# Earlier pieces of a chip kernel's start: one array tile for the first convolution kernels, a shorter VectorE chain, a later x load, and the first Toeplitz rows in two pieces

## What is computed

```python
dt = exp(log_dt); A = -exp(log_A_real) + 1j * A_imag
dtA = A * dt[:, None]
P = dtA[:, :, None] * arange(1024)
Cs = Cc * (exp(dtA) - 1.0) / A
K = 2.0 * einsum('hn,hnl->hl', Cs, exp(P)).real     # filter of 1024 taps for each of 64 channels, 64 modes
y = irfft(rfft(u * mask, 2048) * rfft(K, 2048))[..., :1024] + u * mask * D[:, None]
y = y * mask
x = x + attention(y)
x = x + ffn(x @ W[condition])
```

## Time and profile before

| what | us |
|---|---|
| median of 3 runs | 920.03 |
| lowest and highest | 919.63, 921.61 |
| the profiled execution, its own time | 920.28 |
| its span (first to last instruction) | 918.5 |
| busy in the span: PE | 879.2 (96%) |
| busy in the span: DVE, POOL, ACT | 444.7, 395.0, 202.1 |
| PE at work on the convolution from | 27.3 |
| PE at work on the projections from | 179.2 |

### The profile page before, as it was taken

How to read it: one execution, slowest core, us unless ns; L and a number is a source line. 1 busy time by engine, 2 the same in 40 slices (tenths; PEclk the granted TensorE clock), 3 DMA queues, 4 the chain that set the end, 5 groups by cost and what they waited for, 6 DMA issues and landing times.

```text
span 918.5 us, 24871 instructions
## 1 busy us (share of the span) xinstructions
PE 879.2 (96%) x11040; PEld 765.9 (83%) x11040; DVE 444.7 (48%) x935; ACT 202.1 (22%) x363; POOL 395.0 (43%) x294
## 2 busy tenths in 40 slices
PE   0899999999999999999999999999999999999998
PEld 0789899988888888888777777777789999999997
DVE  7555663111222222248887766788533344333444
ACT  4334552200000000023133222333231111011110
POOL 1244555401565556759978877877521000000000
PEclk9999999999999999999999999999999999999999
DMA  2678877412213322155546463634252221212201
GB/s 65 153 189 205 202 178 185 128 46 69 69 70 92 89 72 69 47 183 155 158 117 178 115 182 115 198 113 139 97 185 95 70 93 47 93 70 70 92 26 69
DMA packets 81930, 105.35 MB, mean 115 GB/s; under 512 B 41504, under 2 KB 54432, under 8 KB 81824
## 3 DMA queue, kind: packets, MB, share of 16 engines
q1 hardware_dynamic: 81312, 103.24, 39.1%
q0 software_dynamic: 512, 0.53, 0.2%
HBM read 74.08 MB, written 29.65 MB: 113 GB/s over the span
## 4 chain that ended last, share of the span: by engine, by line
PE 92%; DMA 2%; DVE 2%; issue 1%; SPq 1%; POOL 1%; ACT 0%; DVEq 0%; POOLq 0%
PE ps L810 24%; PE ps L1262 21%; PE ps L1076 19%; PE ps L529 9%; PE ps L774 5%; PE ps L540 4%; PE ps L1032 3%; PE ps L1012 3%; PE ps L1235 2%; PE ps L1282 1%; DMA kpad<-ksb 1%; PE ps L1283 1%; DMA xc<-in_dram 1%; DMA toep<-kpad 1%; PE ps L460 0%
## 5 line engine op out<-in xcount | busy, mean ns | idle before, releaser
L1262 PE MATMUL ps<-wb,xf 128*128 128x420 f32 (+1 forms) x1152 | 195.2, 329 | 0.0
L1262 PEld LDWEIGHTS ps<-wb,xf 128*128 128x128 f32 x1152 | 189.6, 188 | 2.8 <-issue 0.2
L810 PE MATMUL ps<-y_hi,w_hi 128*128 128x512 f32 x320 | 125.2, 391 | 0.0
L810 PE MATMUL ps<-y_lo,w_hi 128*128 128x512 f32 x320 | 124.6, 390 | 0.0
L810 PE MATMUL ps<-y_hi,w_lo 128*128 128x512 f32 x320 | 124.6, 389 | 0.0
L529 PE MATMUL ps<-xc,toep 64*128 64x192 f32 (+4 forms) x1088 | 100.9, 338 | 12.8 <-DMA toep<-kpad 8.4
L529 PEld LDWEIGHTS ps<-xc,toep 64*128 64x128 f32 x1088 | 92.9, 192 | 17.0 <-issue 12.5
L1076 PE MATMUL ps<-y_hi 128*128 128x512 f32 x256 | 103.9, 406 | 0.2 <-POOL y_lo L945 0.2
L1076 PE MATMUL ps<-y_lo,y_hi 128*128 128x512 f32 x256 | 100.7, 393 | 0.0
L1076 PE MATMUL ps<-y_hi,y_lo 128*128 128x512 f32 x256 | 100.6, 393 | 0.0
L917 POOL TENSOR_TENSOR rot<-rot,cst 128x512 f32<-128x512 f32 x40 | 52.7, 1318 | 73.0 <-DVE rot L888 73.0
(11 more groups left out here) (145 smaller groups left out, 1284.9 us busy)
## 6 DMA issues: line engine op xcount, KB each, us to landing
toep<-kpad SPq DMA_DIRECT2D x64, 272.0 KB, 4.6
xc<-in_dram SPq DMA_DIRECT2D x32, 256.0 KB, 5.0
q_rows<-rf SPq DMA_DIRECT2D x32, 256.0 KB, 2.6
q<-q_rows SPq DMA_DIRECT2D x16, 512.0 KB, 5.0
xr<-in_dram SPq DMA_DIRECT2D x16, 512.0 KB, 4.6
x_scratch<-xr SPq DMA_DIRECT2D x16, 512.0 KB, 3.1
x<-x_scratch SPq DMA_DIRECT2D x16, 512.0 KB, 3.7
out_dram<-x SPq DMA_DIRECT2D x15, 512.0 KB, 2.6
```

Of the source, the lines that this page charges most:

```text
L810: mm = pe.matmul(kq_bank(n), w[a][:, j, :], yt[b][:, j, g * 512:(g + 1) * 512], start=(j == 0 and a + b == 0), stop=(j == NJ - 1 and a == 1))
L1262: mm = pe.matmul(joint_bank(i, piece)[:, 0:hi - lo], xf[i % 2][:, a, t, :], wb[t][:, w4_place(t, c), lo:hi], start=(t == 0 and a + c == 0) ...
```

## The change

Five edits, all in the convolution's first steps.

- `phase_rates`: the negation of `ar` is gone; `rho` is made by one instruction from `ar` and `dt` with the factor -1. `ar` keeps its sign, and later sums and differences are turned accordingly.
- `first_tables`: the two squares of `ar` and of the imaginary part are made by ScalarE, behind `sh` and `ch`; VectorE waits for eight of ScalarE's results rather than six, and has 22 instructions rather than 24.
- group 0 only, `kernels_pe` and `kernels_out`: two matmuls over all 128 rows into bank 6 rather than four over 64 rows into two banks; the addition of bank 7 is gone. The groups from 1 on are as before.
- `load_parameters`: x for n = 0 and 1 is loaded behind the zeros, the skip weights and the lengths.
- `load_toeplitz`: for n = 0 each of the two loads is cut in two at column 576 (`NEAR`): both near pieces first, with a semaphore of their own, then both far pieces. `convolve(0)` begins on the near pieces and waits for the far ones ahead of `narrow`.

```diff
@@ load_parameters
             sp.dma_start(cst[:], consts).then_inc(ld_cst, 16)
-            load_x_conv(sp, 0)
...
             sp.dma_start(len_i[:], lens.partition_broadcast(P)).then_inc(ld_len, 16)
+            load_x_conv(sp, 0)
@@ first_magnitudes_and_sines
             act.activation(M("ch"), M("r"), ACT.Sin, scale=0.4999998, bias=C("half_pi")).then_inc(a_set, 1)
+            act.activation(M("k"), M("ar"), ACT.Square).then_inc(a_set, 1)
+            act.activation(M("t2"), AIM, ACT.Square).then_inc(a_set, 1)
             sines(act, 0)
@@ phase_rates
             v.wait_ge(a_set, 2)
-            chain(v, v.tensor_scalar(M("ar"), M("ar"), -1.0, None, ALU.mult))
-            chain(v, v.tensor_tensor(M("rho"), M("ar"), M("dt"), ALU.mult))
+            chain(v, v.scalar_tensor_tensor(M("rho"), M("ar"), -1.0, M("dt"), ALU.mult, ALU.mult))
@@ first_tables
-            v.wait_ge(a_set, 6)
+            v.wait_ge(a_set, 8)
...
-            v.tensor_tensor(M("k"), M("ar"), M("ar"), ALU.mult)
-            chain(v, v.tensor_tensor(M("t2"), AIM, AIM, ALU.mult))
+            chain(v, v.tensor_tensor(M("k"), M("k"), M("t2"), ALU.add))
             v.scalar_tensor_tensor(M("t0"), M("cm1"), 1.0, M("tanh"), ALU.add, ALU.mult)
             v.tensor_tensor(M("ni"), M("t1"), M("e1"), ALU.mult)
-            chain(v, v.tensor_tensor(M("k"), M("k"), M("t2"), ALU.add))
-            v.tensor_tensor(M("nr"), M("t0"), M("cm1"), ALU.add)
             chain(v, v.reciprocal(M("den"), M("k")))
+            chain(v, v.tensor_tensor(M("nr"), M("t0"), M("cm1"), ALU.add))
@@ kernels_pe
-                for r in range(2):
+                if g == 0:
+                    mm = pe.matmul(ps[:, 6, cols], ltab[:, cols], rtab[:, cols], start=True, stop=True)
+                for r in range(2 if g > 0 else 0):
@@ kernels_out
-            v.tensor_copy(k, low).then_inc(v_kl, 1)
-            v.wait_ge(v_kl, g + 1)
-            v.tensor_tensor(k, k, high, ALU.add).then_inc(v_ke, 1)
+            if g == 0:
+                v.tensor_copy(k, low).then_inc(v_ke, 1)
+            else:
+                v.tensor_copy(k, low).then_inc(v_kl, 1)
+                v.wait_ge(v_kl, g)
+                v.tensor_tensor(k, k, high, ALU.add).then_inc(v_ke, 1)
@@ load_toeplitz
+        NEAR = NJ // 2 * P + HALF
...
+            near = NEAR if n == 0 else 0
+            if near:
+                for r in range(2):
+                    sp.dma_start(toep[r * HALF:(r + 1) * HALF, n % TR, 0:near],
+                                 bass.AP(kpad, head(n, r) * (KROW + 1), [[1, HALF], [1, near]])).then_inc(ld_near, 16)
             for r in range(2):
-                sp.dma_start(toep[r * HALF:(r + 1) * HALF, n % TR, :],
-                             bass.AP(kpad, head(n, r) * (KROW + 1) + 0, [[1, HALF], [1, L + HALF]])).then_inc(ld_toep[n % TR], 16)
+                sp.dma_start(toep[r * HALF:(r + 1) * HALF, n % TR, near:],
+                             bass.AP(kpad, head(n, r) * (KROW + 1) + near, [[1, HALF], [1, L + HALF - near]])).then_inc(ld_toep[n % TR], 16)
@@ convolve
-            pe.wait_ge(ld_toep[n % TR], 16 * 2 * (n // TR + 1))
+            if n == 0:
+                pe.wait_ge(ld_near, 16 * 2)
+            else:
+                pe.wait_ge(ld_toep[n % TR], 16 * 2 * (n // TR + 1))
...
                         mm = wide(pe, n, c, d, start=(d + c == 0))
+                if n == 0:
+                    pe.wait_ge(ld_toep[0], 16 * 2)
```

More of the change, by code:

```diff
@@ L260, in build @@
         st_zero, st_k = signal("st_zero"), signals("st_k", 2 * GP)
+        ld_near = signal("ld_near")
         ld_toep, ld_xc = signals("ld_toep", TR), signals("ld_xc", XR)
@@ L409, in first_tables @@
             phases(v, 0)
-            v.wait_ge(a_set, 6)
+            v.wait_ge(a_set, 8)
+            v.scalar_tensor_tensor(M("cm1"), M("sh"), -2.0, M("sh"), ALU.mult, ALU.mult)
             v.scalar_tensor_tensor(M("tanh"), M("e1"), 1.0, M("tanh"), ALU.add, ALU.mult)
-            v.scalar_tensor_tensor(M("cm1"), M("sh"), -2.0, M("sh"), ALU.mult, ALU.mult)
             v.scalar_tensor_tensor(M("t1"), M("sh"), 2.0, M("ch"), ALU.mult, ALU.mult)
-            v.tensor_tensor(M("k"), M("ar"), M("ar"), ALU.mult)
-            chain(v, v.tensor_tensor(M("t2"), AIM, AIM, ALU.mult))
+            chain(v, v.tensor_tensor(M("k"), M("k"), M("t2"), ALU.add))
             v.scalar_tensor_tensor(M("t0"), M("cm1"), 1.0, M("tanh"), ALU.add, ALU.mult)
             v.tensor_tensor(M("ni"), M("t1"), M("e1"), ALU.mult)
-            chain(v, v.tensor_tensor(M("k"), M("k"), M("t2"), ALU.add))
-            v.tensor_tensor(M("nr"), M("t0"), M("cm1"), ALU.add)
             chain(v, v.reciprocal(M("den"), M("k")))
+            chain(v, v.tensor_tensor(M("nr"), M("t0"), M("cm1"), ALU.add))
+            v.tensor_tensor(M("t1"), M("ni"), AIM, ALU.mult)
             v.tensor_tensor(M("t0"), M("nr"), M("ar"), ALU.mult)
-            v.tensor_tensor(M("t1"), M("ni"), AIM, ALU.mult)
             v.tensor_tensor(M("t2"), M("ni"), M("ar"), ALU.mult)
             chain(v, v.tensor_tensor(M("k"), M("nr"), AIM, ALU.mult))
-            v.tensor_tensor(M("gr"), M("t0"), M("t1"), ALU.add)
-            chain(v, v.tensor_tensor(M("gi"), M("t2"), M("k"), ALU.subtract))
+            v.tensor_tensor(M("gr"), M("t1"), M("t0"), ALU.subtract)
+            chain(v, v.tensor_tensor(M("gi"), M("t2"), M("k"), ALU.add))
             v.tensor_tensor(M("gr"), M("gr"), M("den"), ALU.mult)
@@ L434, in first_tables @@
             chain(v, v.scalar_tensor_tensor(M("k"), M("gr"), 2.0, CIM, ALU.mult, ALU.mult))
-            v.tensor_tensor(M("cr"), M("t0"), M("t1"), ALU.subtract)
-            chain(v, v.tensor_tensor(M("ci"), M("t2"), M("k"), ALU.add))
+            v.tensor_tensor(M("cr"), M("t0"), M("t1"), ALU.add)
+            chain(v, v.tensor_tensor(M("ci"), M("k"), M("t2"), ALU.subtract))
         def tables(v, g):
```

## The result

The changed kernel's median was 915.17 us (911.26 to 920.47, 9 runs) beside 917.82 for the kernel before (916.36 to 921.61, 9 runs): ratio 0.9964 with a 95% interval of 0.9948 to 0.9979. It is faster, by 0.36%: little, but outside the interval's noise. The forecast 917.6 lay 2.4 too high. Against the 920.03 that stood in the first table the gain is 4.86, twice what I forecast.

What follows compares the result with a forecast made beforehand. TensorE, 92% of the critical chain, was taken as the bound, so only an earlier start could help: 0.23 + 0.27 + 0.45 + 1.45 = 2.40 off the 920.03 median gives 917.6 us, range 914.9 to 920.6.

Steps and rivals of the forecast that it cites:

- Part 1: VectorE's rates: folding the negation into rho saves one waited instruction, a gain of 0.23 us.
- Part 2: Group 0's tables: moving two squares from VectorE to ScalarE saves two issue slots, 0.27 us (bounds 0.13 and 0.52).
- Part 3: Group 0's first filters: one bank without the addition gains 0.45 us; the whole-array matmuls themselves count 0.
- Part 4: Loading x behind the small loads at the start: no gain, 0 us.
- Part 5: First Toeplitz rows loaded in two pieces: second near piece lands in 3.22 instead of 4.67 us, gain 1.45.
- the gain passes on: First filters' store: the 0.45 us saved on the addition reaches the store and the Toeplitz issue in full.
- No wait on the far pieces: Convolution start: far pieces and the rows for n = 1 arrive in time, covered by 1.0 and 1.8 us.
- Nothing says that the stall is tied to the old positions: TensorE's stall at 55.63: no evidence that it depends on the old positions, so its vanishing got only chance 0.10.
- the vanished stall: TensorE's 1.94 us stall at 55.63 and its half clock disappear: 913.8, or 915.8 if only the clock stays up; chance 0.10.
- the slower side: Another TensorE stall at L529 grows to 1.9 us and halves the clock, costing 3.3: 920.9; chance 0.15.
- the little split: First Toeplitz landing is mostly fixed, so cutting the load gains 0.5 instead of 1.45 us: 918.6; chance 0.15.
- The shift taken back: Later transfers, not TensorE, set the pace, so the earlier start is lost: 919.5 to 920; chance 0.05.

Runs made afterwards that it cites:

- e5: The changed kernel run once more, with no further edit, beside the kernel before: mean 915.24 +- 0.51 us.
- e13: The changed kernel run a third time, no further edit; no mean of its own given, the changed kernel's four batches together 915.22 +- 0.33 us.
- e18: The changed kernel run again, beside a repeat of the version with 64 idle-time matmuls added: mean 914.90 +- 0.61 us.
- e4: The kernel before with only the first Toeplitz rows loaded in two pieces: mean 918.42 +- 0.66 us.
- e6: The changed kernel with 36 waited VectorE instructions added ahead of the first rate, TensorE's stream untouched: mean 924.12 +- 0.85 us.
- e8: The changed kernel with 32 short matmuls on constants (128 records) added ahead of the first filters: mean 920.38 +- 0.59 us.
- e7: The changed kernel with TensorE's idle time filled by matmuls on constants, 20 ahead of the first filters and 13 behind: mean 915.48 +- 0.63 us.
- e9: The changed kernel with two matmuls on constants (8 records) added in TensorE's idle time ahead of the first filters: mean 916.96 +- 0.41 us.

## Why the prediction was right in its steps and short in its sum

**Part 1**, right: from L378 at 4.33 and L380 at 4.82 to L381 at 4.26 and L382 at 4.52, of which 0.07 is an earlier landing of the parameters; 0.23.

**Part 2**, right: tables of group 0 began at 15.45 before and at 14.88 now, 0.57, less 0.07 and 0.23: 0.27. The slots of 0.13 and 0.26 held, which are the two prices by which a waited operation costs more at 64 columns. The squares took 0.24 each and hid in ScalarE's idle time, 2.06 of which is left.

**Part 3**, right up to the store and 0.33 short behind it. The whole-array matmuls take 1.23 as before, the addition's 0.45 is gone, the store is issued 1.03 earlier. But I wrote that "the gain passes on", and the store's landing, which had not been on the chain, came onto it. I never asked of the first store what its own landing would hold up once it was early.

**Part 4**, right: nothing within the errors.

**Part 5**, right in kind, 0.27 to 0.3 small: the second near piece landed 2.93 after its issue, not 3.22; the wait from the first issue fell from 5.19 to 3.46. The error of part 3 and this one offset by luck: 2.40 forecast, 2.44 in the profile (1.77 in e5, where both the store and the landing were slower; 2.43 in e13, 2.21 in e18).

**No wait on the far pieces**: nearly. The far pieces and the rows for n = 1 were in time; a wait of 0.2 stands ahead of n = 3 (TensorE on the Toeplitz rows, in the changed kernel), where the chain now goes through the filters of group 1.

**What failed** is the step "Nothing says that the stall is tied to the old positions", by which I gave the vanished stall 0.10 and took the unchanged one for the forecast. I had the fact in the words: the stall is the stream's own. In the kernels whose heads differ by 8 records it comes at the same count of the stream, and part 3 alters what work lies at that count. With the length put back the changed kernel is 1.36 +- 0.52 under the one before, somewhat less than its start; the shorter stream brings 2.40 +- 0.59. The sum held the term for this at 0. The rival was nearer than I thought: in eight profiles the stall at 1207 is gone twice and shorter six times, and in all eight the clock stays up behind it, for which the rival had named 915.8. But its reason is not shown to be the whole one, since the convolution as a whole is hardly shorter in these profiles and the rest of the kernel is. The executions at a mean clock of 1.000 go from one in fifty to one in five. For the slower side I took a stall of 1.9 as enough to bring the half clock; the changed kernel's profile has one of 2.19 at 539.78 with the clock at 1.00 behind it. **The second failure** is the base: I set the sum against a median of three runs that lay 1.05 above the mean of 148.

**The other rivals**: the little split is refuted by the start (1.33 earlier in e4, 1.73 less wait in the changed kernel, not 0.5); the time of e4 alone could not have told. The shift taken back is refuted by e6 for a later start, and not tested apart for an earlier one. The slower side did not come by the change, but e8 is a case of it: 5.2 over the changed kernel, 1.1 of it from the start. Which stalls make up the other 4.1 was not isolated.

## What to carry to other kernels

When a change adds or removes instructions of a long unrolled stream, treat the count as a variable of its own: add the same number back in idle time and time that too, before you credit the edit. When a stage is made to start earlier, ask of the transfer that its first result goes through whether it was waited for at all before; it may be now. And take the base from as many executions as the result, since three can be a microsecond off in nine hundred.

## What was not expected of the hardware

- TensorE's stream stalled after the same counts of records in kernels whose heads differ by 8 records: after 1207 in 13 of 15 profiles, after 13385 in all 15. With 256 records more the latter stands after 13641. The longest of these stalls is 2.65 (e7, at 499.39). Behind one of about 2 the granted clock can fall to half: it did behind 1.94, and did not behind 2.14 in e9.
- Executions of one kernel differ by up to 11 us (the kernel before: 913.01 to 924.16), and the mean granted clock explains a good part: fitted over the executions of the kernel before, 0.001 less of mean clock goes with 1.0 us more of span.
- A TensorE kept busy with matmuls on constants began the convolution at the full clock: 32 records in 3.08 rather than 4.86. Short ones of 32 columns did not do this: their 64 records took 13.86, 0.22 each, and the convolution's 32 behind them 4.66.
- The first store landed 0.8 to 1.0 after the end of one 8 KB instruction packet in 19 of 20 profiles, and sooner than all of them (1.4 after its issue) in the one where the packet had passed long before.
